# Selective scan: B and C as 32 rows per pair, spread over the channels by 0/1 products

## The reference, cut to what matters

```python
z = h @ in_w.T                       # [B, T, 64]
gate = silu(h @ gate_w.T)
A = -exp(A_log)                      # [64, 16]
Bi = z @ Bp_w.T                      # [B, T, 16]
Ci = z @ Cp_w.T                      # [B, T, 16]
dt = softplus(z @ dt_w.T + dt_b)
A_bar = 1.0 + dt[..., None] * A
state = a_bar * state + dtz_t[:, :, None] * b_t[:, None, :]   # dtz = dt * z, once per token
y = sum(state * c_t[:, None, :], axis=-1)
return (y * gate) @ out_w.T
```

## Time and profile before

| | |
|---|---|
| median of 3 runs | 2493.7 us (2488.06 to 2498.01) |
| span of the profiled execution | 2493.0 us |
| time of that execution around its span | not given apart; the median is 0.7 us above the span |
| stage of the scan in the trace | 832.3 to 958.9 us, 126.6 us |
| one pair in the steady part | 13.4 us |
| TensorE busy over the whole span | 89% |

### The profile page before, as it was taken

The page is one execution under the profiler, slowest core; times in us unless marked ns, Lnnn a source line. Parts: engine busy times, 40 slices in busy tenths (PEclk is TensorE's granted clock), DMA queues, the critical chain, the costliest instruction groups (busy, mean ns, idle before and its releaser), DMA issues. The chain is left out here.

```text
span 2493.0 us, 48623 instructions
## 1 busy us (share of the span) xinstructions
PE 2221.8 (89%) x17358; PEld 1814.4 (73%) x17360; DVE 1680.9 (67%) x3260; ACT 1318.5 (53%) x3083; POOL 805.3 (32%) x1019
## 2 busy tenths in 40 slices
PE   6979799999699797989999979999779897999875
PEld 5857587887476696778888658888567686788652
DVE  4767544774666586765677646666677785888858
ACT  4558635665477663542666443333476574445335
POOL 4656402333255442100233202222211100544365
PEclk9989879999899898979999999999889999999888
DMA  3000082113400000032211430000200002877711
GB/s 113 2 1 2 1 338 83 52 52 131 147 2 2 22 2 1 2 157 115 100 52 51 163 130 1 2 1 1 102 1 1 1 1 88 229 207 214 230 29 34
DMA packets 102933, 178.37 MB, mean 72 GB/s; under 512 B 59687, under 2 KB 71591, under 8 KB 97578
## 3 DMA queue, kind: packets, MB, share of 16 engines
q1 hardware_dynamic: 85514, 135.93, 16.4%
q0 software_dynamic: 9792, 28.85, 3.6%
q10 hardware_dynamic: 7392, 10.49, 1.2%
HBM read 112.44 MB, written 62.78 MB: 70 GB/s over the span
## 5 line engine op out<-in xcount | busy, mean ns | idle before, releaser
L2356 POOL TENSOR_TENSOR l2a_Pn<-l2a_Pn,l2a_rden 128x1024 f32<-128x1024 f32 x32 | 60.0, 1897 | 288.9 <-DVE l2a_rden L2595 288.9
L1630 ACT ACTIVATE l0f_w_parts<-l0f_W 128x512 fp32r (+1 forms) x117 | 90.4, 775 | 64.8 <-PE l0f_psG L1435 50.4
L1788 DVE TENSOR_TENSOR l0f_w_parts<-l0f_W,l0f_w_parts 128x512 fp32r<-128x512 f32 (+1 forms) x117 | 99.2, 867 | 37.7 <-ACT l0f_w_parts L1630 37.5
L1630 ACT ACTIVATE l1f_w_parts<-l1f_W 128x512 fp32r (+1 forms) x117 | 90.5, 774 | 63.1 <-PE l1f_psG L1435 50.3
L4188 POOL TENSOR_TENSOR l3x_Pn<-l3x_Pn,l3x_fac 128x616 f32<-128x616 f32 (+2 forms) x96 | 70.3, 761 | 150.3 <-DVE l3x_fac L4267 140.6
L1788 DVE TENSOR_TENSOR l1f_w_parts<-l1f_W,l1f_w_parts 128x512 fp32r<-128x512 f32 (+1 forms) x117 | 99.2, 867 | 12.6 <-ACT l1f_w_parts L1630 12.2
L1488 PE MATMUL l1f_psY<-l1f_W,l1f_XT_hT 128*128 (+1 forms) x440 | 104.2, 380 | 0.8 <-ACT l1f_XT_hT L1610 0.8
L883 ACT ACTIVATE l1a_att_Pn<-l1a_att_psS,l1a_att_nmx 128x128 f32<-128x128 f32 x256 | 91.8, 418 | 1.7 <-DVE l1a_att_nmx L1002 1.7
L883 ACT ACTIVATE l0x_Pn<-l0x_psS,l0x_nmx 128x128 f32<-128x128 f32 x256 | 91.7, 418 | 0.9 <-DVE l0x_nmx L1002 0.9
L706 POOL TENSOR_TENSOR l1a_att_Pn<-l1a_att_Pn,l1a_att_rden 128x512 f32<-128x512 f32 x64 | 66.5, 1039 | 72.1 <-DVE l1a_att_rden L1009 72.1
L1488 PEld LDWEIGHTS l1f_psY<-l1f_W,l1f_XT_hT 128*128 128x128 f32 x440 | 80.3, 190 | 10.8 <-issue 1.0
(11 more groups left out here) (883 smaller groups left out, 7652.5 us busy)
## 6 DMA issues: line engine op xcount, KB each, us to landing
relative_rows<-l3x_ext SPq DMA_DIRECT2D x32, 516.0 KB, 5.9
l1f_W<-in_l1f_w SPq DMA_DIRECT2D x9, 1536.0 KB, 20.1
l0f_W<-in_l0f_w SPq DMA_DIRECT2D x8, 1536.0 KB, 26.4
cumulative_rows<-l3x_cum SPq DMA_DIRECT2D x32, 384.0 KB, 3.4
l3x_K<-keys SPq DMA_DIRECT2D x16, 512.0 KB, 5.2
l3x_rel<-relative_rows SPq DMA_DIRECT2D x32, 231.0 KB
values<-l1f_W SPq DMA_DIRECT2D x11, 512.0 KB, 5.6
l3x_V<-values SPq DMA_DIRECT2D x16, 308.0 KB
```

The lines of the kernel that those rows point to most:

```text
L1630: nc.scalar.activation(w_high[i], W[:, bass.ds(act_offsets[k] + o, m)], ACT.Copy).then_inc(high_ready, 1)
L1788: nc.vector.tensor_tensor(w_low[i], W[:, bass.ds(dve_offsets[k] + o, m)], w_high[i], ALU.subtract).then_inc(low_ready, 1)
L2356: nc.gpsimd.tensor_tensor(part, part, rden[b % 2][:, 8 * u:8 * u + 8].unsqueeze(2).to_broadcast([P, 8, P]), ALU.mult)\
```

## The change

B and C are first computed once per pair as 2 x 16 rows of states instead of 128 channels. `states_by_row` makes two products with a 128x128 matrix each, in which the 2 x 16 columns of weights stand four times, so that the same 32 rows appear in each quarter of the partitions. ScalarE copies both results (128x256) to `bc`. `to_channels` then spreads them: `pick` is a matrix of zeros and ones, and a product of 32 rows of it with 32 rows of `bc` puts one state's row under all 64 channels of both batches. Four products in a row use four different quarters of the partitions and four different banks of `psB`. Halves `h` are no longer apart: `inputs(p)` waits for both `weigh` of the pair before, `outputs(p)` for both `drive`. GpSimd builds `pick` at the start of the stage with a memset and four `affine_select`. The tables of B and C in DRAM shrink from 2 x 1 MB to 128 KB.

```diff
-    inw, gatew, dtw, dtb, outw, alog, nw, bdB, bdC = (L.t[n] for n in (...))
+    inw, gatew, dtw, dtb, outw, alog, nw, bcw = (L.t[n] for n in (...))
+    bc = [R.sb(f"bc{i}", [P, 2 * P]) for i in range(2)]
+    pick = R.sb("pick", [P, ST // 4 * P])
...
+        step.do(nc.gpsimd.memset(pick[:, :], 0.0))
+        pick4 = pick[:, :].rearrange("p (q i c) -> p q i c", q=ST // 4, i=2)
+        for r in range(4):
+            step.do(nc.gpsimd.affine_select(out=pick4, in_=pick4, compare_op=ALU.not_equal, fill=1.0, base=-(32 + ST // 4) * r,
+                                            pattern=[[-1, ST // 4], [-ST, 2], [0, SC]], channel_multiplier=1))
+        nc.gpsimd.memset(G.pad[:, 7:8], 0.0).then_inc(picks_ready, 1)
...
         def transpose_x(p):
             pe.wait_ge(xn_ready, p + 1)
             past(pe, hT_ready, p)
+            past(pe, bc_ready, p)
...
-        def inputs(p, h):
-            past(pe, weighted, 2 * (p - 1) + h + 1 if p else 0)
-            for s in range(h * HS, (h + 1) * HS):
-                ins = nc.tensor.matmul(psB[:, s * P:(s + 1) * P], bdB[:, s * P:(s + 1) * P], zg[p % 2][:, 0:P], start=True, stop=True)
-            ins.then_inc(b_done, 1)
-
-        def outputs(p, h):
-            pe.wait_ge(u_ready, 2 * p + h + 1)
-            for s in range(h * HS, (h + 1) * HS):
-                ins = nc.tensor.matmul(psB[:, s * P:(s + 1) * P], bdC[:, s * P:(s + 1) * P], zg[p % 2][:, 0:P], start=True, stop=True)
-            ins.then_inc(c_done, 1)
+        def states_by_row(p):
+            pe.wait_ge(z_ready, p + 1)
+            pe.wait_ge(hT_ready, p + 1)
+            for k in range(2):
+                ins = nc.tensor.matmul(psX[:, k * P:(k + 1) * P], bcw[:, k * P:(k + 1) * P], zg[p % 2][:, 0:P], start=True, stop=True)
+            ins.then_inc(bc_done, 1)
+
+        def to_channels(p, k):
+            for q in range(ST // 4):
+                for r in range(4):
+                    rows, s = slice(32 * r, 32 * r + 32), ST // 4 * r + q
+                    ins = nc.tensor.matmul(psB[:, s * P:(s + 1) * P], pick[rows, q * P:(q + 1) * P], bc[p % 2][rows, k * P:(k + 1) * P],
+                                           start=True, stop=True)
+            return ins
+
+        def inputs(p):
+            pe.wait_ge(bc_ready, p + 1)
+            past(pe, weighted, 2 * p)
+            to_channels(p, 0).then_inc(b_done, 1)
+
+        def outputs(p):
+            pe.wait_ge(u_ready, 2 * p + 2)
+            to_channels(p, 1).then_inc(c_done, 1)
...
             nc.scalar.activation(av[:, :], psZ[:, 2 * P:3 * P], ACT.Abs, bias=dtb[:, 0:1]).then_inc(abs_ready, 1)
+            act.wait_ge(bc_done, p + 1)
+            past(act, c_done, p - 1)
+            nc.scalar.activation(bc[p % 2][:, :], psX[:, 0:2 * P], ACT.Copy).then_inc(bc_ready, 1)
             act.wait_ge(abs_ready, p + 1)
```

More of the change, by code:

```diff
@@ L1982, in scan_loads @@
     parts = [(n, [P, size], F32, A["l1s_" + n]) for n, size in (("in", DC * SC), ("gate", DC * SC), ("dtw", P), ("dtb", 1), ("out", D), ("Alog", ST),
-                                                             ("norm", DC), ("B", ST * P), ("C", ST * P))]
+                                                             ("norm", DC), ("BC", 2 * P))]
     return "scan", Loads(nc, G, "scan_w", parts)
@@ L1992, in selective_scan @@
     L = G.ready.pop("scan")
-    inw, gatew, dtw, dtb, outw, alog, nw, bdB, bdC = (L.t[n] for n in ("in", "gate", "dtw", "dtb", "out", "Alog", "norm", "B", "C"))
+    inw, gatew, dtw, dtb, outw, alog, nw, bcw = (L.t[n] for n in ("in", "gate", "dtw", "dtb", "out", "Alog", "norm", "BC"))
     loaded, NL = L.loaded, L.count()
@@ L2017, in selective_scan @@
         "b_done", "u_ready", "c_done", "scanned", "weighted", "sum_done", "yT_ready", "y_done", "x_ready"))
+    picks_ready, bc_done, bc_ready = (R.sem(n) for n in ("picks_ready", "inputs_outputs_done", "inputs_outputs_ready"))
     dt_ready, dtz_ready, rg_ready, gate_ready, abar_act, abar_pool, summed = (R.sem(n) for n in (
@@ L2113, in _ @@
         step_sizes(0)
+        states_by_row(0)
+        pe.wait_ge(picks_ready, 1)
         for p in range(NP2):
@@ L2116, in _ @@
                 transpose_x(p + 1)
-            inputs(p, 0)
-            inputs(p, 1)
+            inputs(p)
             if p:
@@ L2122, in _ @@
                 project(p + 1)
-            outputs(p, 0)
+            outputs(p)
             if p + 1 < NP2:
                 step_sizes(p + 1)
-            outputs(p, 1)
+                states_by_row(p + 1)
             if p:
@@ L2157, in _ @@
             past(act, dtz_ready, p - 1)
-            past(act, c_done, 2 * (p - 1))
+            past(act, bc_done, p - 1)
             nc.scalar.activation(zg[p % 2][:, :], psZ[:, 0:2 * P], ACT.Copy).then_inc(z_ready, 1)
@@ L2210, in drive @@
         def drive(p, h):
-            dve.wait_ge(b_done, 2 * p + h + 1)
+            dve.wait_ge(b_done, p + 1)
             dve.wait_ge(dtz_ready, p + 1)
@@ L2230, in weigh @@
             dve.wait_ge(scanned, 2 * p + h + 1)
-            dve.wait_ge(c_done, 2 * p + h + 1)
+            dve.wait_ge(c_done, p + 1)
             nc.vector.tensor_tensor(half(u[p % 2], h), half(st, h), half(psB, h), ALU.mult).then_inc(weighted, 1)
@@ L4347, in blocks, with states @@
     return out.reshape(P, -1)
+def states(w):
+    out = np.zeros((P, 4, 2, ST), w.dtype)
+    for i in range(2):
+        out[i * SC:(i + 1) * SC, :, i, :] = w[:, None, :]
+    return out.reshape(P, P)
 def more_layout(I, A):
@@ L4357, in more_layout @@
     A["l1s_out"], A["l1s_Alog"] = twice(I["L1_attn_out_w"].T), twice(I["L1_attn_A_log"])
-    A["l1s_B"], A["l1s_C"] = (blocks(np.repeat(I[f"L1_attn_{n}p_w"].T[:, :, None], SC, axis=2)) for n in "BC")
+    A["l1s_BC"] = np.concatenate([states(I[f"L1_attn_{n}p_w"].T) for n in "BC"], axis=1)
     A["l1s_norm"] = cols(I["L1_attn_norm2_w"])
@@ L4400, in used_inputs @@
     if "l1a" in t:
-        names |= {"l1s_" + n for n in ("in", "gate", "dtw", "dtb", "out", "Alog", "B", "C", "norm")}
+        names |= {"l1s_" + n for n in ("in", "gate", "dtw", "dtb", "out", "Alog", "BC", "norm")}
     if "l2x" in t:
```

## The result

The changed kernel takes 2504.83 us (median of 4, 2498.16 to 2507.09), the kernel before 2491.69 in the same session (2488.06 to 2498.01). The ratio is 1.0040, with a 95% interval from 1.0022 to 1.0057: slower by 0.2 to 0.6%. That is a loss. The ratio lies within the 0.5% that the prediction counts as no change, but the median lies 1.8 us above the top of its range. Twelve runs of the changed kernel in a later session gave 1.0022 (1.0008 to 1.0036), eleven in a third 1.0039 (1.0025 to 1.0053). The profiled execution here is the fastest of its four.

What follows compares the result with a forecast made beforehand. TensorE was taken to pace the steady pair, VectorE next. From 2493.0 us, -3.6 without the clock and +4.0 for it gave 2493.4; with the median 0.7 above the profile's span, 2494, range 2485 to 2503.

Steps and rivals of the forecast that it cites:

- What bounds the kernel: In the steady pair TensorE, busy all 13.44 us, sets the pace; VectorE's own row is the next bound at 12.1 us.
- Spread: Each spread of B or C on TensorE takes 1.3 us (1.05 to 1.8), switching included, instead of 3.74.
- Serial quarters (D): Rival: weight loads of the four quarters go one after another; pair 1.9 us longer, 2508 us; chance 0.07.
- The wait on `add_y`: `sum_states` now waits for `add_y`; `gate_y` still starts 0.69 us earlier per pair, -5.2 us over seven waits.
- Full gain (E): Rival: `gate_y`'s full 1.34 us wait is won per pair, `add_y` being met earlier; 2484 us; chance 0.06.
- the prediction's sum without the clock: Over the stage: -5.2 for shorter `gate_y` waits, +1.0 for scans meeting GpSimd, +0.6 at the start, so -3.6 us.
- Start of the stage: First pair: uncovered copy and two products on a cold TensorE delay `dt`, +0.6 us (0.4 to 1.2); `pick` hidden.
- ScalarE's chain: The next pair's step size, with the new copy, is ready 0.55 us before VectorE asks for it: covered.
- Scans against GpSimd: Earlier scans meet GpSimd's work for 0.3 us, at 0.27 us per us plus a stretched addition: +1.0 us.
- TensorE's clock: Idle TensorE's clock falls once per pair, costing 0 to 1.73 us; a third taken, 0.57, over seven pairs +4.0 us.
- C, 2502: Rival: the low clock covers the sum in every pair, 8 us more than the forecast; chance 0.12.

## Why the prediction came out as it did

- **What bounds the kernel**: right. TensorE paced the pair, and with enough of it removed VectorE's own row is the bound: 12.35 us where nothing waits.
- **Spread**: 1.17 us of matmuls, 0.98 of loads, with 0.17 of switching ahead; the forecast was 1.3 with the switching. Serial quarters (D) are out.
- **The wait on `add_y`**: right at the full clock, sum 0.73 us held back, `gate_y` 0.75 left, pair 12.91. Full gain (E) is out for this order. With the clock kept up, the time to the seventh `gate_y` is 107.5 us, 3.2 less than before (110.7); the prediction's sum without the clock was -3.6.
- **Start of the stage**: forecast +0.6, up to the end of the first pair's second `weigh`. That comes 24.08 us after the stage's start, against 24.00 and 23.62 in two executions of the kernel before, so +0.1 to +0.5. `dt` came 0.46 later, the first `drive` waited another 0.85 for a spread at half clock, and the first scans met less of GpSimd's work (5.58 us instead of 6.13). The first `gate_y`, for which the prediction had a gain of 1.1 besides, came 0.45 later instead (30.75 after 30.30), as the spread and the sum ahead of it ran in part at half clock; with the clock up it came 1.1 earlier (29.20).
- **ScalarE's chain**: covered; `dt` waits only in the first pair. `pick`, four selects in 3.11 us, is hidden.
- **Scans against GpSimd**: this term was mis-sized. In the changed kernel it hardly came to bear, 4.46 us as before, because `gate_y` was late. With the clock up it is 4.54; but moved by another 0.75 us (the addition first), it was 5.80, so the scans lost 1.3 us where 0.27 us per us gives 0.2. In the rows the loss does not grow with the time for which the engines meet: it is about the length of the addition, all at once, where the addition begins during the first scan, and little where it begins with the second. The rate of 0.27 came from a misread row: in the first pair of the kernel before the addition (851.48) began only in the second scan, which took 2.48 us; the excess lay in the first (3.73 us), beside GpSimd's product for `abar`, which ran until 849.12.
- **TensorE's clock**: the step that failed, in its size. That the level falls once in each pair was right. The term was "a third of it, 0.57 per pair, 7 x 0.57 = +4.0", of bounds 0 and 1.73, and the third was a choice, not a reading. It measured 0.72 in the steady pairs of three executions and 2.0 to 2.3 in those of two, above the upper bound, since that came from a sum that was only in part at half clock (5.47 us; in the long pattern it took up to 6.79). Up to the seventh `gate_y` that is 5.0 us against the run with the clock kept up in the short pattern, 13.8 and 12.8 in the two long ones, where the prediction has 4.0. The prediction held the low stretch on the sum in every pair for a rival (C, 2502); it is one of two patterns in which the same kernel runs. With two in five at about +10.4 in the stage and three at +1.6, the mean is +5.1, against +0.4 in the prediction's sum (-3.6 + 4.0).

The forecast of 2494 was thus low by some 5 us for what the stage shows. The three ratios are worth 5.5 to 10 us, so the stage accounts for between half of the difference and nearly all of it. What the rest is stays open: outside the stage the span is 2365.0, 2365.0 and 2357.9 us in three profiled executions with the kernel before's order of TensorE, and 2366.8, 2359.0, 2366.5, 2367.3 and 2367.5 in the five of the changed one. That hints at 2 or 3 us more, but the scatter is as large, and six executions with parts of the change or more than it have 2361.6 to 2366.3. The two sublayers behind the scan don't hold it: together they take 528.6 to 529.3 us in the three profiled executions first named and 527.7 to 531.7 in the five of the changed kernel. A cause was not tried. How often each pattern comes can't be said from five executions, and what sets it neither.

## What to carry to other kernels

Work taken off the engine that paces a loop is worth only what the next bound gives, here 0.5 of 13.4 us for some 4 us of work; and if it leaves TensorE idle for a couple of us in each round, the clock can charge more than that. So before shortening TensorE's work read the windows for where the idle time will be and which row stands behind it: the low stretch is cheap over idle time, dear over the product that another engine waits for, and it may land on either from one execution to the next. Then take away the next limits together: here clock, VectorE's order and GpSimd's addition beside the scans gave 0.4% against the kernel before as a set, while with the clock alone, the order alone, or these two, the ratio stayed between 0.9986 and 1.0012, with intervals that reach 1.

## What the hardware showed that was not expected

- The same program with the same data ran its loop at 13.63 us per pair in three executions and at 14.2 to 15.9, longer and shorter in turn, in two, by where and for how long TensorE's clock was low (3.4 us a pair in the one pattern, 6.8 in most pairs of the other).
- A GpSimd addition of 128x512 that begins during the first of VectorE's two scans costs both engines: 3.25 us instead of 1.27, and 5.80 instead of 4.46. One that begins with the second scan is as slow itself (3.26), but costs the scans little (4.68). (The Trainium skill's "GPSIMD Engine Reference", section "Specifications", says that GpSimd shares its SBUF interfaces with VectorE and names contention with VectorE's instructions that have two inputs in SBUF, as these scans have; the trace agrees, and puts the price at about 2 us for the one and 1.3 for the other.)
- 16 matrix products of 32 rows by 128 columns in float32 (32 records), in four quarters and four banks in turn, take 1.17 us at 2.4 GHz and 2.09 at 1.2 GHz.
